# A recurrence of 512 steps: rounds of 32 steps written out in place of inner loops on three engines

## The reference, cut to what matters

```python
def cell(h, x):
    gi = x @ W_ih + b_ih
    gh = h @ W_hh + b_hh
    i_r, i_z, i_n = jnp.split(gi, 3, axis=-1)
    h_r, h_z, h_n = jnp.split(gh, 3, axis=-1)
    r = jax.nn.sigmoid(i_r + h_r)
    z = jax.nn.sigmoid(i_z + h_z)
    n = jnp.tanh(i_n + r * h_n)
    h_new = (1.0 - z) * n + z * h
    return (h_new, h_new)
_, hs = jax.lax.scan(cell, initial_state, xs)   # 512 steps, 4 rows of 512
```

## Time and profile before

| what | value |
|---|---|
| median of three executions | 3966.25 us (3960.25 to 3973.56) |
| the profiled execution | 3962.8 us, its span 3961.1 us |
| instructions in the span | 169,151 |
| TensorE busy | 3673.0 us, 93% |
| VectorE busy | 2291.8 us, 58% |
| ScalarE busy | 1502.0 us, 38% |
| POOL busy | 525.1 us, 13% |
| mean granted clock of TensorE | 0.974 of full speed |

### The profile page before, as it was taken

One profiled execution on the slowest core, in us unless ns is written; L12 is line 12 of the kernel. 1 busy time (PEld: TensorE's weight loads), 2 busy tenths in 40 slices (PEclk: granted clock), 3 DMA queues, 4 the chain that ended last, 5 costly groups with the idle time before them and its releaser, 6 DMA issues. The chain is left out here.

```text
span 3961.1 us, 169151 instructions
## 1 busy us (share of the span) xinstructions
PE 3673.0 (93%) x68991; PEld 2358.3 (60%) x68991; DVE 2291.8 (58%) x6130; ACT 1502.0 (38%) x5279; POOL 525.1 (13%) x1107
## 2 busy tenths in 40 slices
PE   7999999999999999999799999868899998949989
PEld 3788888888888888887444444424333333525554
DVE  2566666666666666666577777734566664413338
ACT  0344444444444444444344444422444443201110
POOL 0111111101111111100122222200000000731110
PEclk9999999999999999999999999989999998979999
DMA  3910000000000000001111111020111121259977
GB/s 113 360 70 0 0 0 0 0 0 0 0 0 0 0 0 0 0 0 32 55 57 37 54 39 37 19 77 32 57 56 56 56 75 41 74 157 304 303 230 297
DMA packets 148323, 266.07 MB, mean 67 GB/s; under 512 B 23977, under 2 KB 77365, under 8 KB 144290
## 3 DMA queue, kind: packets, MB, share of 16 engines
q1 hardware_dynamic: 115874, 204.00, 14.9%
q10 hardware_dynamic: 18976, 43.01, 4.1%
q0 software_dynamic: 13408, 18.20, 1.3%
HBM read 148.41 MB, written 89.39 MB: 60 GB/s over the span
## 5 line engine op out<-in xcount | busy, mean ns | idle before, releaser
L318 PE MATMUL gru_prz<-ahead,h 128*4 128x160 f32 x16384 | 748.0, 300 | 9.8 <-DVE h L436 9.8
L318 PE MATMUL gru_pn<-ahead,h 128*32 128x128 f32 x16384 | 636.9, 273 | 0.0
L318 PEld LDWEIGHTS gru_pn<-ahead,h 128*32 128x32 f32 x16384 | 491.0, 110 | 35.2
L318 PEld LDWEIGHTS gru_prz<-ahead,h 128*4 128x4 f32 x16384 | 387.1, 87 | 147.4 <-DVE h L436 20.5
L417 DVE STREAM_TRANSPOSE gru_tr<-gru_prz 128x160 f32<-128x160 f32 x512 | 179.2, 350 | 467.7 <-PE gru_prz L318 467.7
L318 PE MATMUL gru_pz<-ahead,h 128*4 128x96 f32 x16384 | 433.3, 246 | 4.6 <-issue 4.6
L373 ACT ACTIVATE gru_rn<-gru_pre 128x16 f32<-128x16 f32 x512 | 119.7, 234 | 746.0 <-DVE gru_pre L420 746.0
L318 PEld LDWEIGHTS gru_pz<-ahead,h 128*4 128x4 f32 x16384 | 363.6, 87 | 6.7 <-issue 5.3
L279 POOL COPY gru_pick<-ident 128x4 f32 x512 | 96.5, 189 | 1374.1 <-PE gru_pz L311 1368.2
L950 DVE TENSOR_REDUCE da_mx<-da_ps 128x2 f32<-128x1024 f32 (+3 forms) x256 | 201.3, 817 | 130.8 <-PE da_ps L643 130.8
L436 DVE TENSOR_TENSOR_SCAN h<-gru_d 128x16 f32<-128x16 f32 (+1 forms) x1024 | 236.1, 231 | 51.9 <-ACT gru_d L380 0.9
(11 more groups left out here) (312 smaller groups left out, 5791.4 us busy)
## 6 DMA issues: line engine op xcount, KB each, us to landing
ahead<-in_L_ffn_gate_up_proj SPq DMA_DIRECT2D x64, 768.0 KB, 6.5
yk<-gru_zeros SPq DMA_DIRECT2D x6, 4096.0 KB, 35.5
ex_wd<-in_L_ffn_down_proj ACTq DMA_DIRECT2D x64, 384.0 KB, 5.7
ahead<-yk SPq DMA_DIRECT2D x16, 1536.0 KB, 9.2
xg<-gru_zeros SPq DMA_DIRECT2D x4, 4224.0 KB, 30.5
ex_xg<-xg ACTq DMA_DIRECT2D x64, 264.0 KB, 5.7
ahead<-wide SPq DMA_DIRECT2D x15, 1024.0 KB, 4.7
ahead<-xnT SPq DMA_DIRECT2D x15, 1024.0 KB, 4.5
```

The source lines that it names most:

```text
L318: last = nc.tensor.matmul(rows(j), of(c), whh[:, c, j, cols], start=False, stop=True, skip_group_check=True)
```

## The change

The inner loops over `c` on TensorE and VectorE, and the inner loop over the 32 steps on ScalarE, become loops of the program that writes the kernel: their turns are written out one behind the other. The body of the loop over `kb` then holds 32 steps on each of the three engines. `c` and `n` become constants, so that `kb` alone is still counted in a register. The operations, their order on each engine, their data and their semaphores stay the same.

```diff
@@ TensorE
             with pe.Fori(0, NBL - 1) as kb:
-                with pe.Fori(0, NG) as c:
+                for c in range(NG):
                     for k in range(KD):
                         s = kb * 32 + c * KD + k
                         add_z_input(s, k % 2)
@@ ScalarE
             with act.Fori(0, NBL) as kb:
-                with act.Fori(0, 32) as n:
+                for n in range(32):
                     step(kb * 32 + n, kb)
@@ VectorE
             with dve.Fori(0, NBL - 1) as kb:
-                with dve.Fori(0, NG) as c:
+                for c in range(NG):
                     for k in range(KD):
                         if k == 0:
                             dve.wait_ge(gi_out, kb * NG + 1)
```

## The result

The changed kernel takes 4078.66 us (median of 4, 4069.77 to 4080.63) against 3964.77 us before: ratio 1.0273, 95% interval 1.0258 to 1.0287, so 114 us slower. The forecast was 4075 us, 109 us slower. The profiled execution has a span of 4078.9 us.

The account below looks back on a forecast made before the run. The prediction took a ring of dependent operations, 3.40 us a step, to bound the kernel. Terms -30.5, +80, +42 and +20 gave +111 us on the profiled 3962.8, hence 4075 us; range 3955 to 4600.

Parts of the forecast that it names:

- The round end: At 14 round ends TensorE's jump waits 3.7 us for code, slow clock adds 2.9, old cost 0.86 goes: +80 us.
- The first round: In the first round, new TensorE code under the zero fill takes 7.31 us a packet instead of 3.76: +42 us.
- The back-edges: Inside rounds, 105 TensorE back-edges of the loop over c go, 0.29 us each: -30.5 us.
- Late packets: In later rounds some TensorE instruction packets come late: 0.05 us x 29 packets x 14 rounds, +20 us.
- rivals 1 and 2: Quiet stretches: fetches not quite keeping up, about 4460 us, chance 0.20; or every fetch taking 7.31 us, about 5,460, chance 0.10.
- The jumps of VectorE and ScalarE costed at nothing: At round ends these engines' jumps to new code run beside TensorE's and are shorter: no cost.
- The count of packets: On TensorE's instruction queue q8, about 41 + 14 x 29 = 447 packets, the same number in every round.
- Rival 3: At round ends, TensorE's store holds the new body or the jump's fetch is early: 3965 us, or 3924; chance 0.14.

Follow-up runs that it names:

- Experiment 5: Kernel before, with TensorE's fifteen rounds written out without a loop over kb; ScalarE and VectorE keep their loops: 3986.45 us, ratio 1.0039.
- Experiment 3: Changed kernel, with the zero fill issued in the last round behind the loads of the next weights: 4052.57 us, ratio 1.0201 to the kernel before.
- experiment 1: Kernel before, with only TensorE's inner loop of 32 steps written out; VectorE and ScalarE keep their inner loops: 4083.13 us, ratio 1.0293.
- experiment 2: Kernel before, with only VectorE's and ScalarE's inner loops written out; TensorE keeps its loop of four steps: 3997.59 us, ratio 1.0067.
- Experiment 8: Kernel before, with TensorE looping over two rounds and thirteen written out without a jump, and the zero fill after eight steps: 3939.04 us, ratio 0.9916.
- experiment 6: Kernel before, with TensorE's inner loop holding eight steps per turn in place of four: 4322.46 us, ratio 1.0888.

## Why the prediction was right, point by point

**The round end** was the main term and it held: +80 forecast, +81.1 and +77.8 measured, 14 times. Its parts are there, but their sizes are off and the errors cancel. The forecast also names the clock after a stop in GHz; no row or run shows that, and the traces give the clock only as a share of full speed: 0.56 over the 6.6 us of rows 8 (0.50 in each microsecond from 120.60 to 125.60), and 0.54 at the round end shown. At this round end, the step and the one behind it take 9.29 + 4.16 = 13.45 us, 6.65 over two plain steps: 3.97 of waiting and 2.7 of slower work. In the mean of fourteen, the wait was priced at 3.7 us and measured 4.2 (59.0 / 14). What is left of 81.1 / 14 + 0.75 = 6.5 us for the slow clock and all else is 2.3, by difference, where 2.9 was priced. And 0.75 us came off for the old round end, not 0.86, since the step before it still takes 3.52. That the sum came within 0.1 us a round is in part luck. Experiment 5 took the jump away and the term vanished.

**The first round**, +42 against +38.0, came from counting packets at 7.31 us each until the fill ends. The queue of the changed kernel shows the count: 14 packets from 110 to 211 us, and 14 in the 50 us behind.

```profile
q8 instruction: 14, 0.23, 0.8%
...
q8 instruction: 14, 0.23, 1.9%
```

That is 7.2 us and 3.6 us a packet. Experiment 3 took the fill away and the term vanished.

**The back-edges** were worth what was said. Outside the first round there are 14 x 7 = 98 of them, 98 x 0.29 = 28.4 us. In experiment 5, 29 of the 434 steps inside fourteen rounds last over 3.5 us where before had 3.40 (or 3.52 just ahead of a round's end), some 8 us in all; the others are as short as plain steps were, at the former back-edges too. The 20.5 us saved and the 8 us late make 28.5.

**Late packets** were the loosest term, forecast at 20 us. By difference they cost 28.4 - 23.5 = 5 us in the first profile of the change and 11 in the second, but 15 in experiment 3 (with -13.6) and 22 in experiment 1 (with -6.6). The term was a guess per packet on a margin of 0.1 us, and it differs that much from run to run. Still, this settles rivals 1 and 2, which had 0.30 together: in experiment 5, 366 packets move on q8 from 300 to 1700 us, and the late ones cost some 8 us in all. That holds with no other DMA; under the zero fill new code is dear (1,828 products in the 101 us that hold 3,257 without it).

**The jumps of VectorE and ScalarE costed at nothing** was the step that failed in its reason, though it hardly moved the sum. The cover that I named, line 417's wait of 0.94 us and ScalarE's wait of 1.36 us, is shorter than their stops of 3.2 and 2.5 us; experiment 2 prices them at 1.5 us a round. In the change it is TensorE's own longer stop, in the same place, that covers most of them. At the start of the last round TensorE leaves its loop while ScalarE jumps back once more, under the load of the next weights: ScalarE's stop of 8.02 us stands open and is the +8.3 that I did not foresee. I had not followed ScalarE's loop through all of its 16 rounds. Where ScalarE keeps its loop, TensorE's own stop of 5.36 us there costs nearly as much (+7.8, experiment 1); I had not priced that either.

**The count of packets** was to be 447 and is 498. The size of a packet held. The forecast took 253 loads and products between two stops and rounded them up to some 256 instructions, 1.10 steps, for waits and register operations that no row shows. Experiment 5 writes out 480 steps where the kernel before has a body of four, 476 more, for 467 - 41 = 426 more packets: 1.12 steps or 255 loads and products each. Experiment 8 writes out 13 x 32 = 416 more for 413 - 41 = 372: 1.12 steps again. The change has 498 - 467 = 31 more than the run without a jump, 2.2 for each of 14 jumps. They may be code read ahead past the end of the loop, or the packets at its two ends, of which only a part belongs to the body; no run tells these apart.

**Rival 3** (the body stays, or the jump is cheap) fell by the largest margin: a quarter of the body does not stay either. In the kernel before at least 1,360 loads and products lay in TensorE's store, and experiment 6 shows that a body of 1,824, with its waits, is fetched anew each turn, 8.9 packets a turn. Its 3924 us had no cost at a jump and the code of the first round ahead of the fill; the change jumps back in each round and meets the fill. The runs tell the two apart: with TensorE's rounds written out without a jump but under the fill the kernel is 0.4% slower (experiment 5), and only with the fill moved off new code is it 0.8% faster (experiment 8, with the first two rounds still looped).

The sum was closer than its terms: the recurrence lost 103 to 109 us where 111 was forecast, because the late packets (15 or 9 us too many) covered the last round (8 too few). That is luck, as the 5 to 22 us of the late packets show. The 14.6 us behind the recurrence, which the forecast did not have, are no more than those stages scatter.

## What to carry to other kernels

Before writing out a loop, count its instructions: here 912 loads and products were kept and 1,824 were not. As long as TensorE kept the body, a back-edge cost a fraction of a microsecond (0.29 here); once it did not, each jump back cost 5 us or more of waiting and slow clock, whether the body was two or eight times as long as the one that was kept. Then either keep the loop small, or go all the way to code without a jump, which cost almost nothing here in a stretch without other transfers (some 8 us for 366 packets, experiment 5). And keep bulk transfers off any stretch in which an engine runs code for the first time: moving the fill took the first round from 38.0 us longer than before to 9.7 us shorter (experiment 3).

## What was not expected of the hardware

- TensorE kept a loop of 912 loads and products and did not keep one of 1,824, although that is only 7.2 packets of code: 60 turns of it cost more (4322 us) than 15 turns of a body four times as long (4083 us, experiment 1).
- Each jump back made TensorE fetch about 2.2 packets of 16 KB more than the same code without a jump (498 packets against 467).
- New code behind a loop can be as dear as a jump where other transfers run: 5.36 us on TensorE at 1907.64 in experiment 1, under the load of the next weights. The kernel before has no such step there, only one of 3.83 us two steps before the last round begins; the code for the first two steps of its last round had come by 147 us, beside the loop that was kept.
